# A block-diagonal matmul operand laid out with its blocks outermost, and its raw input loaded one slot ahead

## The reference

```python
x0 = x
xk = x
outs = []
for W in (W0, W1):
    Hk = xk.shape[1]
    Hn = W.shape[-1]
    Wr = W.reshape(m, Hk, Hn)
    xk = jnp.einsum('bid,bjd,ijh->bhd', x0, xk, Wr)
    outs.append(xk)
result = jnp.concatenate(outs, axis=1)
return jnp.sum(result, axis=-1)
```

## Time and profile before

| | |
|---|---|
| Time, median of 3 runs | 781.15 us (778.26 to 783.33) |
| The profiled execution's own time | 786.45 us |
| Its span, first to last instruction | 784.2 us |
| Mean granted TensorE clock | 0.882 |
| Busy: TensorE matmuls, weight loads | 616.8 us (79%), 533.2 us (68%) |
| Busy: VectorE, ScalarE, GpSimd | 469.4 us (60%), 468.3 us (60%), 460.2 us (59%) |
| Moved by DMA | 150.77 MB in 128374 packets, mean 192 GB/s |

### The profile page before, as it was taken

How to read it: one execution, slowest core, us unless ns; L and a number is a source line. 1 busy time by engine, 2 the same in 40 slices (tenths; PEclk the granted TensorE clock), 3 DMA queues, 4 the chain that set the end, 5 groups by cost and what they waited for, 6 DMA issues and landing times.

```text
span 784.2 us, 12914 instructions
## 1 busy us (share of the span) xinstructions
PE 616.8 (79%) x3176; PEld 533.2 (68%) x3176; DVE 469.4 (60%) x806; ACT 468.3 (60%) x980; POOL 460.2 (59%) x404
## 2 busy tenths in 40 slices
PE   3476677988797787988669878779877778877888
PEld 2365566877686676877557767668766667676778
DVE  5466576676665665676446756466765655755630
ACT  4557675676665565676446766456675555765640
POOL 6667675676565566566464666465665555665610
PEclk9897898999888888989789999898998899888999
DMA  8966666676555665565564655665655765546410
GB/s 295 330 228 217 229 233 222 199 248 224 164 163 162 219 223 188 176 200 184 179 222 143 193 186 186 217 196 174 217 182 160 234 211 147 207 138 221 130 29 14
DMA packets 128374, 150.77 MB, mean 192 GB/s; under 512 B 79792, under 2 KB 88368, under 8 KB 128304
## 3 DMA queue, kind: packets, MB, share of 16 engines
q1 hardware_dynamic: 128304, 149.94, 59.2%
HBM read 137.30 MB, written 4.65 MB: 181 GB/s over the span
## 4 chain that ended last, share of the span: by engine, by line
PE 30%; DMA 29%; SPq 18%; ACT 10%; issue 8%; DVE 4%; ACTq 1%; DVEq 0%
DMA xdr<-xd_dram 28%; SPq L271 11%; PE acc L362 6%; PE acc L363 4%; PE acc L364 4%; ACT fh L456 4%; SPq L237 4%; PE fin L403 3%; PE pg L389 2%; PE pg L391 2%; PE fin L404 2%; PE pg L390 2%; PE fin L405 2%; ACT x L477 2%; ACT xl L463 2%
## 5 line engine op out<-in xcount | busy, mean ns | idle before, releaser
L693 POOL TENSOR_TENSOR fl<-fs,fh 128x512 fp32r<-128x512 f32 x192 | 246.2, 1292 | 99.1 <-ACT fh L456 98.9
L362 PE MATMUL acc<-fh,w0h 128*128 128x512 f32 x384 | 178.5, 465 | 124.4 <-ACT x L477 110.8
L593 DVE TENSOR_TENSOR fl<-fp,fh 128x512 fp32r<-128x512 f32 x192 | 132.0, 688 | 199.4 <-ACT fh L456 198.0
L362 PEld LDWEIGHTS acc<-fh,w0h 128*128 128x128 f32 x384 | 80.1, 209 | 147.9 <-ACT x L477 71.3
L688 POOL TENSOR_TENSOR fs<-xr,xs 128x512 f32<-128x512 f32 x128 | 162.4, 1291 | 5.8 <-DMA xr<-xb_dram 5.8
L363 PE MATMUL acc<-fh,w0l 128*128 128x512 f32 x384 | 164.7, 429 | 0.0
L364 PE MATMUL acc<-fl,w0h 128*128 128x512 f32 x384 | 163.9, 427 | 0.0
L589 DVE TENSOR_TENSOR fp<-xl,xr 128x512 f32<-128x512 f32 x192 | 133.6, 697 | 39.3 <-ACT xl L463 30.0
L607 DVE TENSOR_TENSOR gl<-pg,gh 128x320 fp32r<-128x320 f32 x256 | 119.1, 486 | 47.0 <-ACT gh L496 43.0
L456 ACT ACTIVATE fh<-fp 128x512 fp32r<-128x512 f32 x192 | 113.8, 592 | 54.9 <-PE acc L364 52.8
L697 POOL TENSOR_TENSOR xdhl<-xdr,xdhl 128x160 fp32r<-128x160 f32 x64 | 34.0, 532 | 183.7 <-ACT xdhl L484 183.6
(11 more groups left out here) (38 smaller groups left out, 797.0 us busy)
## 6 DMA issues: line engine op xcount, KB each, us to landing
xr<-xb_dram SPq DMA_DIRECT2D x192, 512.0 KB, 4.9
xs<-xa_dram SPq DMA_DIRECT2D x64, 256.0 KB, 5.6
xbd<-xdhl SPq DMA_DIRECT2D x512, 20.0 KB, 2.4
xp<-xpairs_dram SPq DMA_DIRECT2D x32, 256.0 KB, 3.7
xdr<-xd_dram SPq DMA_DIRECT2D x64, 80.0 KB, 6.2
w_copy<-w_dram SPq DMA_DIRECT2D x6, 384.0 KB, 6.3
w1l<-w_copy SPq DMA_DIRECT2D x6, 384.0 KB, 5.3
out_dram<-outs SPq DMA_DIRECT2D x8, 256.0 KB, 7.5
```

Of the source, the lines that this page charges most:

```text
L362: nc.tensor.matmul(acc[:, :], w0h[:, t, :], fh[:, t, :], start=t == 0, stop=False)
L593: nc.vector.tensor_tensor(fl[:, t, :], f_at(t), fh[:, t, :], ALU.subtract).then_inc(low_dve, 1)
L693: nc.gpsimd.tensor_tensor(fl[:, t, :], f_at(t), fh[:, t, :], ALU.subtract).then_inc(low_pool, 1)
```

## The change

`xbd` gets the block index b as its outermost free dimension, so that what one block DMA writes in a partition is one piece of 320 elements (1280 B) where it was 8 pieces of 40 (160 B). The matmuls therefore read 8 runs of 40 columns at a distance of 320 elements, and write `pg` as 8 runs of 40 at a pitch of 64 elements instead of 320 contiguous ones; the evictions read `pg` at that pitch, still a quarter at a time. `xdr` gets two buffers with a semaphore each, and its load of group g+2 follows directly on the blocks of g. The load of the first third of `xr` goes ahead of the blocks. The wait for the split of g now stands at the head of SyncE's slot. `final_out` goes from behind the high parts to right behind `x1_out` on ScalarE.

```diff
-        xdr = sb("xdr", [P, NQ, MI])
+        xdr = sb("xdr", [P, 2, NQ, MI])
         xdhl = sb("xdhl", [P, 2, NQ, 2, MI], F32R)
-        xbd = sb("xbd", [P, 2, NQ, 2, BQ, MI], F32R)
+        xbd = sb("xbd", [P, 2, BQ, NQ, 2, MI], F32R)
...
         def g_psum(odd, q):
+            rows = pg[:, q % 2, :].rearrange("p (b i) -> p b i", b=BQ)[:, :, 0:MI]
             if odd:
-                return pg[:, q % 2, 0:BQ * MI].rearrange("p (b i) -> p i b", b=BQ)
-            return pg[:, q % 2, 0:BQ * MI].rearrange("p (b u r) -> p u r b", b=BQ, r=IB)
+                return rows.rearrange("p b i -> p i b")
+            return rows.rearrange("p b (u r) -> p u r b", r=IB)
...
-            def load_xd(g):
-                sp.dma_start(xdr[:, :, :], xd[g]).then_inc(xd_in, 16)
+            def load_xd(g, gi):
+                sp.dma_start(xdr[:, gi % 2, :, :], xd[g]).then_inc(xd_in[gi % 2], 16)
...
                 for b in range(BQ):
                     rows = slice(D * b, D * b + D)
-                    sp.dma_start(xbd[rows, s, :, :, b, :].rearrange("p q s i -> p (q s) i").bitcast(F32),
-                                 xdhl[rows, s, :, :, :].rearrange("p q s i -> p (q s) i").bitcast(F32))\
+                    sp.dma_start(xbd[rows, s, b, :, :, :].rearrange("p q s i -> p (q s i)").bitcast(F32),
+                                 xdhl[rows, s, :, :, :].rearrange("p q s i -> p (q s i)").bitcast(F32))\
                       .then_inc(xbd_in[s], 16)
...
-                    blocks(g, gi, first, last and gi == CB - 1)
+                    sp.wait_ge(xd_low, g + 1)
                     if more3:
                         wait_product(sp, g + 1, 0)
                         wait_product(sp, g + 1, 1)
                         load_right(j, gi + 3, 0)
+                    blocks(g, gi, first)
+                    if more2:
+                        load_xd(g + 2, gi)
...
-                    if more2:
-                        sp.wait_ge(xd_low, g + 2)
-                        load_xd(g + 2)
...
-            load_xd(0)
+            load_xd(0, 0)
+            load_xd(1, 1)
...
-                o = pg[:, q % 2, 0:BQ * MI]
-                xh = xbd[:, s, q, 0, :, :].rearrange("p b i -> p (b i)")
-                xlo = xbd[:, s, q, 1, :, :].rearrange("p b i -> p (b i)")
+                o = pg[:, q % 2, :].rearrange("p (b i) -> p b i", b=BQ)[:, :, 0:MI]
+                xh, xlo = xbd[:, s, :, q, 0, :], xbd[:, s, :, q, 1, :]
...
                     if prev:
                         x1_out(g - 1, first and gi == 1)
+                    if gi == 1 and not (first or second):
+                        final_out(j - 2)
...
-                    if gi == 1 and not (first or second):
-                        final_out(j - 2)
```

More of the change, by code:

```diff
@@ L158, in build @@
         sq_ready = sem("sq_ready")
-        xd_in = sem("xd_in")
+        xd_in = [sem("xd_in0"), sem("xd_in1")]
         xd_high = sem("xd_high")
@@ L258, in w1_load, with blocks @@
                 sp.dma_start(w1l[:, piece(p), :].bitcast(F32), w1_copy[:, piece(p), :]).then_inc(w1_in, 16)
-            def blocks(g, gi, first, alone):
-                if alone:
-                    sp.wait_ge(xd_low, g + 1)
+            def blocks(g, gi, first):
                 if first and gi < 2:
@@ L329, in _ @@
             load_right(0, 2, 1)
-            sp.wait_ge(xd_low, 1)
-            load_xd(1)
             wait_product(sp, 0, 4)
@@ L480, in xd_split @@
                 g = CB * j + gi
-                act.wait_ge(xd_in, 16 * (g + 1))
+                act.wait_ge(xd_in[gi % 2], 16 * nth(j, gi))
                 if not fresh:
                     act.wait_ge(xbd_in[gi % 2], 16 * BQ * (nth(j, gi) - 1))
-                nc.scalar.activation(xdhl[:, gi % 2, :, 0, :], xdr[:, :, :], COPY).then_inc(xd_high, 1)
+                nc.scalar.activation(xdhl[:, gi % 2, :, 0, :], xdr[:, gi % 2, :, :], COPY).then_inc(xd_high, 1)
             def turned_high(g):
@@ L569, in _ @@
             g_high_part(NCH - 1, CB - 2, 0, True, None)
-            g_high_part(NCH - 1, CB - 2, 1, True, None)
-            g_high_part(NCH - 1, CB - 2, 2, True, None)
-            g_high_part(NCH - 1, CB - 2, 3, True, None)
+            for q in range(1, NQ):
+                g_high_part(NCH - 1, CB - 2, q, True, None)
             turned_high(NG - 1)
@@ L672, in _ @@
             chunk(NCH - 1, False, True, True)
-            for q in range(NQ):
-                g_low_part(NCH - 1, CB - 2, q, True)
+            for u in range(NQ):
+                g_low_part(NCH - 1, CB - 2, u, True)
             turned_low(NG - 1)
-            for q in range(NQ):
-                g_low_part(NCH - 1, CB - 1, q, True)
+            for u in range(NQ):
+                g_low_part(NCH - 1, CB - 1, u, True)
         @block.gpsimd
@@ L696, in xd_split @@
                 pool.wait_ge(xd_high, g + 1)
-                nc.gpsimd.tensor_tensor(xdhl[:, gi % 2, :, 1, :], xdr[:, :, :], xdhl[:, gi % 2, :, 0, :],
+                nc.gpsimd.tensor_tensor(xdhl[:, gi % 2, :, 1, :], xdr[:, gi % 2, :, :],
+                                        xdhl[:, gi % 2, :, 0, :],
                                         ALU.subtract).then_inc(xd_low, 1)
@@ L725, in chunk @@
                         w1_low_part(gi - 1)
-            nc.gpsimd.memset(xbd[:, :, :, :, :, :].rearrange("p u q s b i -> p (u q s b i)").bitcast(F32), 0.0)\
+            nc.gpsimd.memset(xbd[:, :, :, :, :, :].rearrange("p u b q s i -> p (u b q s i)").bitcast(F32), 0.0)\
               .then_inc(xbd_zero, 1)
```

## The result

| | before | after |
|---|---|---|
| Median of the runs of both on one chip | 780.68 us (778.26 to 783.33) | 615.76 us (613.03 to 618.37) |
| The profiled execution's own time, its span | 786.45, 784.2 us | 613.03, 610.8 us |
| Mean granted TensorE clock | 0.882 | 0.989 |
| Sum of waits of ScalarE for xdr | 156.0 us, 34 times | 0.5 us, once |

The ratio after to before is 0.7886, 95% interval 0.7836 to 0.7937. The forecast was 598 us, in a range of 578 to 660; the measurement lies 17.8 us (3%) above the forecast and inside the range.

The account below looks back on a forecast made before the run. The late xdr transfer, behind block DMAs and loads in SyncE's queue, bounded the kernel. Head 21.2, seven slots 66.5, 56 slots 484.4 and tail 28.2 made 600.3, plus 2.25 is 602.5, less 0.7% is 598 us; range 578 to 660.

Parts of the forecast that it names:

- 56 slots: TensorE's work between successive L357 matmuls, after the first seven such slots: 8.65 us each, 484.4 us together.
- the wait goes: ScalarE's wait for xdr before its split (L484), 156.0 us in 34 waits, disappears with the early load.
- 2 us or so to spare if block issue stays at 0.64: Margin of xdr's landing before ScalarE's split if block DMAs get no quicker to issue; otherwise about 4 us.
- The blocks are issued 3.6 us into it: SyncE starts the block DMAs 3.6 us after the start of TensorE's slot, before and after the change.
- I take 0.33 plus the 0.04 between issues: Block DMA issue on SyncE falls from 0.60 to 0.33 us with 1280 B pieces, saving 2.1 us a slot.
- SyncE then is no limit, 6.2 us: SyncE's blocks and loads take 6.2 us a slot, against TensorE's 8.63.
- 8.4, just under: SyncE's issue time per slot in us if blocks stay at 0.64 each, against TensorE's 8.63.
- xdr is still late: Rival: block issue stays at 0.64, xdr lands 0.5 to 2.1 us late, costing 73 us: 671; chance 0.07.
- another load (xs, xr) in front of which ScalarE waits: Sign that the forecast is wrong: ScalarE or GpSimd waits each slot for a load other than xdr.
- the rival's price: Rival: TensorE's strided PSUM writes of pg take two clocks per column, adding 101 us: 698; chance 0.10.
- The rival of slow evictions: Rival: ScalarE's reads of pg at pitch 64 slow from 0.43 to 1.5 us or more, making the kernel slower; chance 0.03.
- L403's 32.6 us of waits go: TensorE's six waits at L403 for ScalarE's output copy vanish because the copy moves up behind x1.

Follow-up runs that it names:

- two-load kernel: The changed kernel with the right operand loaded as two DMAs of three tiles instead of three of two, same bytes: 601.33 us, ratio 0.7648.
- written-out kernel: The changed kernel with the chunk loops of all engines written out, no loop at all: 590.97 us, ratio 0.7539.
- The probe: The changed kernel with 20 more SyncE DMAs at its end, four in each of five shapes, to measure issue times: 618.22 us, one run.

## Why the prediction came out as it did

**The sum, term by term** (spans, in us):

| | forecast | measured |
|---|---|---|
| Head to the first slot | 21.2 | 21.3 |
| First seven slots | 66.5 | 66.0 |
| 56 slots | 484.4 (8.65 each) | 496.8 (8.87 each) |
| Tail | 28.2 | 26.7 |
| Span | 600.3 | 610.8 |

The miss lies in the 56 slots, +12.4. By the distances of the squares' matmuls (L354), 15 slots of the change exceed 8.65 by 0.15 to 1.75 us, 11.9 together, and in 14 of them ScalarE had waited for xs; the slot of the loop's turn exceeds it by 4.3 and one at 95.7, which is there in the two-load and the written-out kernel too, by 1.1; the others give back 5.0, of which 4.0 are the slots outside the loop, most taking 8.43 to 8.47. That gain was not in the forecast either, so part of its nearness is luck. With the other terms the span is 10.5 above the forecast. The rest of the 17.8 us, some 7, is the step from the profiled execution to the median: the forecast took off 4 us because the median of before lay 0.7% below its profiled execution, and here it lies 2.7 above.

**The early load: right.** The term "the wait goes" held: 156.0 to 0.5 us. The landing of xdr, 6.2 us in the median in the earlier trace rows, was put at 2 to 4:

```profile
DMA to landing us min/median/max: 1.9/2.5/7.2
```

The "2 us or so to spare if block issue stays at 0.64" is near what came: 1.7 us in the median from the landing to ScalarE's split. One term of it was wrong all the same. "The blocks are issued 3.6 us into it" held only where SyncE's queue is not late: in groups 16 to 47 of the change they start 6.1 us into the slot, 3.7 in the written-out kernel. That the transfer took 2.5 us, near the low end of its bounds, made up for a part of it, which is luck. The early load without the new layout shows that it does not need the pieces.

**Pieces of 1280 B: the step that failed.** "I take 0.33 plus the 0.04 between issues" measured 0.59 for the issue and 0.63 from one to the next, as before (0.60 and 0.64):

```profile
L269 SPq DMA_DIRECT2D xbd<-xdhl x512: 507/589/1569, 19.8 to 583.7; - x171
```

The near row was badly chosen: all the DMAs of 0.33 to 0.35 us in the earlier trace rows differ from the blocks in more than one respect, one run per partition, 128 partitions and a source in HBM, and I credited the first. The probe shows that it is neither of the first two: copies of one run per partition take 0.58 to 0.60 us with 16 and with 128 partitions. What is left is where the two ends lie. And in the written-out kernel even a load is issued in 0.43 us, so 0.33 was no lower bound where no register work stands between. Hence "SyncE then is no limit, 6.2 us" was wrong as well, and the figure in brackets beside it, "8.4, just under", right: 8.45 measured. I had not drawn from it that a queue just under the slot has next to no reserve.

**The rival "xdr is still late"** had its condition met, issue at 0.64, but the wrong victim and price: xdr stands right behind the blocks and was in time; xs, further back, was late, and all ragged slots together cost 11.9 us, 0.2 a slot, where the rival had 1.3. The last of the signs named as wrong, "another load (xs, xr) in front of which ScalarE waits", is the one that showed, 22 times.

**The loop's turn: missing from the sum.** Slots of 8.65 throughout left out that TensorE, ScalarE and VectorE jump back once in the 56. Timeline of the change:

```profile
300.94 0.60 ACT L473 ACTIVATE x<-acc 128x512 f32<-128x512 f32 x1 [2.61 <-issue]
...
301.12 0.41 PE L385 MATMUL pg<-xbd,x1th 128*128 128x320 f32 x1 [3.16 <-issue]
...
301.57 0.70 DVE L584 TENSOR_TENSOR fp<-xl,xr 128x512 f32<-128x512 f32 x1 [4.34 <-issue]
```

Each stood still for 2.6 to 4.3 us with nothing to wait for; the two-load kernel has the same slot (13.11), the written-out one has none.

**PSUM: zero, as taken.** The strided writes of pg, timeline of a quick slot of the change:

```profile
181.92 0.31 PE L385 MATMUL pg<-xbd,x1th 128*128 128x320 f32 x1
182.07 0.31 PE L386 MATMUL pg<-xbd,x1th 128*128 128x320 f32 x1
182.22 0.31 PE L387 MATMUL pg<-xbd,x1tl 128*128 128x320 f32 x1
```

They follow each other at 0.15 us as in the earlier trace rows, so the rival's price (598 and 101, which is 699 and not 698) was not paid. The rule of the Trainium skill that the prediction weighed ("PSUM — Partial Sum Buffer", Specifications (TRN2)) is not borne out for runs of 40 words at a pitch of 64. The evictions, in the groups by form, are those of the earlier trace rows, 434 ns:

```profile
L492 ACT ACTIVATE gh<-pg 128x320 fp32r<-128x320 f32 x256 | 106.3, 434 | 22.2 <-PE pg L387 21.5
```

The rival of slow evictions is thus out, and with it the only slower case.

**The output copy: right that it costs nothing,** but "L403's 32.6 us of waits go" was mostly not its doing: with the copy put back only 5.8 us return, and the time stays.

## What to carry to other kernels

Before an edit is credited with shortening an operation, find a row that differs from it in the one thing that the edit changes; if the near rows differ in more than one, take both ends, and work out what the kernel does at the dear one. When the late transfer is mended, add up the whole queue for a period and compare it with the bound engine's: here 16.9 us against 17.2, with issues now and then longer, meant that the lateness went to another load in the queue, and putting that load earlier only passed it on, while one issue less, or cheaper issues, ended it.

## What the runs showed of the hardware that was not expected

- The issue of a DMA from SyncE took 0.58 to 0.60 us with both ends in the on-chip memory, 0.52 with both in HBM, 0.33 to 0.43 from HBM to the chip and 0.36 the other way. Within the on-chip memory 16, 32 and 128 partitions made no difference, and eight pieces of 160 B or one of 1280 B made 0.60 and 0.59.
- A change of kind shows one DMA late: the first load after copies took 581 ns, the next ones 415 to 420.
- In a queue of SyncE without recorded waits some 30 of 430 issues took 0.1 to 1.1 us longer than the usual one, 14 us together in 289; the reason was not found.
- One turn of the chunk loop held TensorE, ScalarE and VectorE for 2.6 to 4.3 us and made that slot 4.3 us longer, at a granted clock of 0.87 in it; and the same slot of TensorE takes 8.62 us inside the loop and 8.43 in written-out code. The two quick slots of the earlier trace rows, 8.63 and 8.47, agree with this. What in the loop costs the 0.2 us was not tried.
